# Output projections of a cross-attention layer as three products of two-part operands, with a new order of the work around them

## The reference, cut to what matters

```python
# first layer, 16 heads of width 16
y = ln(x);  x = x + softmax(q(y) k(y)^T * 64**-0.5) v(y) @ Wo1 + bo1       # self-attention
y = ln(x);  x = x + softmax(q(y) k(ctx)^T * 64**-0.5) v(ctx) @ Wo2 + bo2   # attention to the context
h, g = split(ln(x) @ Wff1 + bff1)                                         # 2 x 1024 columns
x = x + (h * (g * sigmoid(1.702 * g))) @ Wff2 + bff2
# second layer, one head of width 256, keys and values from the context
a = softmax((x @ Wq + bq) (ctx @ Wk + bk)^T / 16) (ctx @ Wv + bv) @ Wfc + bfc
out = norm_w * (x + a) * rsqrt(mean((x + a)**2) + 1e-8)
```

## Time and profile before

| | us |
|---|---|
| runs | 743.69, 746.25, 746.22; median 746.22 |
| profiled execution, its own time | 746.0 |
| its span, first to last instruction | 743.6 |
| TensorE busy | 658.1 (89%) |
| VectorE busy | 541.3 (73%) |
| ScalarE busy | 487.8 (66%) |
| GpSimd busy | 99.2 (13%) |

### The profile page before, as it was taken

How to read it: one execution, slowest core, us unless ns; L and a number is a source line. 1 busy time by engine, 2 the same in 40 slices (tenths; PEclk the granted TensorE clock), 3 DMA queues, 4 the chain that set the end, 5 groups by cost and what they waited for, 6 DMA issues and landing times.

```text
span 743.6 us, 11160 instructions
## 1 busy us (share of the span) xinstructions
PE 658.1 (89%) x4072; PEld 317.0 (43%) x4072; DVE 541.3 (73%) x929; ACT 487.8 (66%) x853; POOL 99.2 (13%) x152
## 2 busy tenths in 40 slices
PE   3989799999999999999999886778799999999981
PEld 2644122222222222222224333425458888888870
DVE  6678989999999999999993637736853944344367
ACT  3543389999999999999998662547374233332374
POOL 2071710000000000000000201345110110000004
PEclk9999699999999999999999997989999999999995
DMA  9448350202020110100000021021000000000003
GB/s 304 182 138 280 96 203 1 72 1 71 2 72 2 33 41 1 30 2 29 2 2 1 14 92 39 17 86 45 2 2 1 0 1 1 1 1 1 1 0 113
DMA packets 35113, 36.87 MB, mean 50 GB/s; under 512 B 6132, under 2 KB 28276, under 8 KB 34804
## 3 DMA queue, kind: packets, MB, share of 16 engines
q1 hardware_dynamic: 33904, 35.87, 14.7%
q0 software_dynamic: 1024, 0.24, 0.3%
q10 hardware_dynamic: 132, 0.07, 0.0%
HBM read 23.09 MB, written 12.74 MB: 48 GB/s over the span
## 4 chain that ended last, share of the span: by engine, by line
PE 63%; DVE 18%; ACT 11%; issue 5%; DMA 1%; POOL 1%; SPq 0%; ACTq 0%; DVEq 0%; POOLq 0%
PE ps L935 15%; PE ps L923 10%; DVE mm L1560 7%; PE ps L719 6%; ACT probs L1318 5%; PE ps L1121 4%; PE ps L752 4%; PE ps L1122 4%; PE ps L1123 4%; PE ps L896 3%; PE ps L705 2%; DVE tok L1538 2%; PE ps L727 2%; PE ps L1038 2%; PE ps L1137 2%
## 5 line engine op out<-in xcount | busy, mean ns | idle before, releaser
L1318 ACT ACTIVATE probs<-ps,unfit 128x512 f32<-128x512 f32 x512 | 311.3, 691 | 29.0 <-PE ps L923 24.2
L1560 DVE TENSOR_REDUCE mm<-ps 128x2 f32<-128x1024 f32 x256 | 299.5, 1220 | 13.8 <-PE ps L752 9.8
L923 PE MATMUL ps<-stack 50*128 50x512 f16 x512 | 146.9, 388 | 7.1 <-ACT probs L1318 1.2
L935 PE MATMUL ps<-probs,v 128*32 128x512 f32 x1024 | 137.3, 608 | 2.6 <-ACT outT L1323 2.6
L752 PE MATMUL ps<-stack 48*128 48x512 f16 x512 | 108.6, 391 | 12.6 <-DVE mm L1560 6.6
L923 PEld LDWEIGHTS ps<-stack 50*128 50x128 f16 x512 | 36.9, 93 | 172.4 <-ACT probs L1318 164.4
L1418 ACT ACTIVATE early<-ps,cols 128x512 f32<-128x512 f32 x32 | 22.0, 688 | 89.8 <-PE ps L1123 89.8
L1819 DVE SCALAR_TENSOR_TENSOR hid<-ps,cols,early 128x512 f32<-128x512 f32 x32 | 24.0, 750 | 72.2 <-PE ps L1123 72.2
L1373 ACT ACTIVATE probs<-ps,unfit 96x1024 f32<-96x1024 f32 x32 | 35.5, 1109 | 34.2 <-PE ps L1029 34.1
L612 POOL TENSOR_TENSOR x<-x,rows 128x512 f32<-128x512 f32 x24 | 31.9, 1340 | 150.6 <-DVE tok L1538 150.5
L1121 PE MATMUL ps<-x_hi,wff_hi 128*128 128x512 f32 x128 | 51.4, 401 | 0.0
(11 more groups left out here) (168 smaller groups left out, 868.9 us busy)
## 6 DMA issues: line engine op xcount, KB each, us to landing
v_groups<-early SPq DMA_DIRECT2D x8, 512.0 KB, 3.4
stack<-q_parts SPq DMA_DIRECT2D x64, 64.0 KB, 2.0
v<-v_groups SPq DMA_DIRECT2D x8, 512.0 KB, 4.0
x<-in_x SPq DMA_DIRECT2D x4, 512.0 KB, 7.7
q_parts<-probs SPq DMA_DIRECT2D x8, 256.0 KB, 3.8
k_parts<-probs SPq DMA_DIRECT2D x8, 256.0 KB, 2.5
stack<-k_parts SPq DMA_DIRECT2D x16, 128.0 KB, 2.5
stack<-q_parts SPq DMA_DIRECT2D x64, 32.0 KB, 1.8
```

Source lines behind the costliest of these rows:

```text
L923: eng.matmul(ps[:, st_bank(n), :], stack[rows_of(tile, KROWS), SLOTS + slot, q, P * kc:P * kc + P], qs[rows_of(tile, KROWS), slot, half, q ...
L935: mm_ = eng.matmul(ps[32 * h:32 * h + 32, PV, :], v1[:, G % 2, kc, 32 * h:32 * h + 32], probs[:, k % 2, h, :], start=(kc == 0), stop=(kc = ...
L1318: eng.activation(probs[:, k % 2, HEADS[h], :], ps[:, st_bank(n), :], ACT.Exp, scale=unfit[:, 0:1]).then_inc(exp_done, 1)
L1560: eng.tensor_reduce(dst, ps[:, 2 * slot:2 * slot + 2, :], AX.X, ALU.max).then_inc(s_red, 1)
```

## The change

- Products: the attended values are kept as a high part (att_hi, written by the ACT copies in fp32r) and a low part (att_lo, a new subtraction on DVE, attended_low, which reads the turn's PSUM banks). The two output weights are split into high and low parts on POOL (wo_split). A tile is then six fp32r products instead of two in fp32. The low parts lie over p1T, so p1T is cleared later, after the last y of the attentions is added. A turn now waits for the subtraction that reads the banks before it.
- Norm: tick() takes a count. A chain's tile calls tick(4) once (before: tick() of four steps up to four times, one of them after the yield); reduce_2 and attended_2 call tick(2).
- Order: the start of the context attention on DVE interleaves the pieces of chain(0, 1) with the first reduces; three set-up products come earlier (SETUPS); load_max_2(2) comes ahead of two stores.
- Tail: the final scaling of blocks 1 to 3 is one DVE operation per tile; ACT and POOL do block 0 alone; the roots of blocks 2 and 3 are computed together; the order of turns, squares and exponentials changes, and the last block is sent before block 2.

```diff
-        attT = (wkv1, wkv2)
...
+        att_hi = [over(f"att_hi{i}", t, [P, NC, BLK], F32R) for i, t in enumerate(("wkv1", "wkv2"))]
+        att_lo = [over(f"att_lo{i}", "p1T", [P, NC, BLK], F32R, NC * BLK * 4 * i) for i in range(2)]
+        wo_hi = [over(f"wo_hi{i}", "early", [P, NC, D], F32R, (5 * NC * D + (4 + 2 * i) * D) * 4) for i in range(2)]
+        wo_lo = [over(f"wo_lo{i}", t, [P, NC, D], F32R) for i, t in enumerate(("wo1", "wo2"))]
...
-        SETUPS = {(2, 3): 1, (3, 1): 1, (3, 3): 1, (4, 0): 1, (7, 0): 1, (7, 1): 2, (7, 2): 1, (7, 3): 1}
+        SETUPS = {(2, 2): 1, (2, 3): 2, (3, 1): 1, (7, 0): 1, (7, 1): 2, (7, 2): 1, (7, 3): 1}
...
             load_max_2(1)
+            load_max_2(2)
             for u in range(half, half + NC):
                 store_parts(u)
-            load_max_2(2)
...
-            for blk in range(BLOCKS):
-                if blk < BLOCKS - 1:
-                    eng.wait_ge(l_out, TPB * (blk + 1))
+            for n, blk in enumerate((0, 1, BLOCKS - 1, 2)):
+                if n == 0:
+                    eng.wait_ge(l_out, TPB)
                 else:
-                    eng.wait_ge(l_last, TPB)
+                    eng.wait_ge(l_last, TPB * n)
...
-            alone(eng.memset(p1T[:, :, :], 0.0))
...
+                    for s in range(2):
+                        eng.wait_ge(v_out[s], 16 * TILES // 4)
+                    for i, w in enumerate((wo1, wo2)):
+                        eng.wait_ge(w_in[("wo1", "wo2")[i]], 16)
+                        eng.tensor_copy(wo_hi[i][:, :, :], w[:, :, :]).then_inc(wo_split, 1)
+                        eng.wait_ge(wo_split, 2 * i + 1)
+                        eng.tensor_tensor(wo_lo[i][:, :, :], w[:, :, :], wo_hi[i][:, :, :].bitcast(F32), ALU.subtract).then_inc(wo_split, 1)
...
-            for blk in range(BLOCKS - 1):
-                for i in range(TPB * blk, TPB * blk + TPB):
-                    eng.wait_ge(l_scaled, i + 1)
-                    eng.tensor_tensor(x[:, i, :], x[:, i, :], rows[:, ROW_W, :], ALU.mult).then_inc(l_out, 1)
+            eng.wait_ge(y_added, 2 * TILES)
+            eng.memset(p1T[:, :, :], 0.0).then_inc(p1T_clear, 1)
+            for i in range(TPB):
+                eng.wait_ge(l_scaled, i + 1)
+                eng.tensor_tensor(x[:, i, :], x[:, i, :], rows[:, ROW_W, :], ALU.mult).then_inc(l_out, 1)
...
                     eng.wait_ge(turn_done, 2 * k)
+                    eng.wait_ge(att_lo_done, BLOCKS * n + 2 * b + (blk % 2 if phase in (ATT1, ATT2) else 2))
...
-                turned(att, 2 * b + 1)
+                eng.wait_ge(att_lo_done, BLOCKS * n + 2 * b + 2)
...
                     for c in range(NC):
-                        mm_ = eng.matmul(ps[:, out_bank(k), 0:D], attT[i // TPB][:, c, P * t:P * t + P], w[:, c, :],
-                                         start=(c == 0), stop=(c == NC - 1))
+                        hi, lo = (v[i // TPB][:, c, P * t:P * t + P] for v in (att_hi, att_lo))
+                        eng.matmul(out, hi, wo_hi[n][:, c, :], start=(c == 0), stop=False)
+                        eng.matmul(out, hi, wo_lo[n][:, c, :], start=False, stop=False)
+                        mm_ = eng.matmul(out, lo, wo_hi[n][:, c, :], start=False, stop=(c == NC - 1))
...
+            l1_turn(last)
             l1_weigh(2)
-            l1_turn(last)
...
+            l1_squares(0)
             l1_turn_copy(2)
-            l1_squares(0)
             l1_exps(last)
+            l1_turn_copy(last)
             l1_squares(1)
-            l1_turn_copy(last)
             l1_scale(0)
             l1_squares(2)
-            l1_scale(1)
             l1_squares(last)
-            l1_scale(2)
...
+            def attended_low(n, blk):
+
+                eng.wait_ge(turn_done, 2 * TURNS.index(((ATT1, ATT2)[n], blk)) + 2)
+                eng.tensor_tensor(att_lo[blk % 2][:, :, :], ps[:, CHAIN:CHAIN + NC, :], att_hi[blk % 2][:, :, :].bitcast(F32),
+                                  ALU.subtract).then_inc(att_lo_done, 1)
+
             def chain(n, b):
-                for _ in range(2):
+                for i in range(2):
+                    attended_low(n, 2 * b + i)
                     yield
                 for i in range(KC):
                     blk, t = divmod(KC * b + i, TPB)
                     add(n, KC * b + i)
-                    tick()
                     if t > 0:
                         eng.wait_ge(y_added, TILES * n + KC * b + i)
                         stats(n + 1, blk, t - 1)
-                        tick()
...
-                    tick()
+                    tick(4)
                     yield
-                    tick()
...
             reduce_2(0, 0)
+            advance(after_self, 1)
             reduce_2(0, 1)
             attended(2 * GROUPS - 1, MISC)
-            after_self, after_cross = chain(0, 1), chain(1, 0)
             reduce_2(0, 2)
+            advance(after_self, 1)
             reduce_2(0, 3)
-            advance(after_self, 4)
+            advance(after_self, 2)
...
+            def l1_final(blk, roots):
+                eng.wait_ge(l_root, roots)
+                for t in range(TPB):
+                    y = x[:, TPB * blk + t, :]
+                    eng.scalar_tensor_tensor(out=y, in0=y, scalar=rms[:, blk, t:t + 1],
+                                             in1=rows[:, ROW_W, :], op0=ALU.mult, op1=ALU.mult).then_inc(l_last, 1)
...
-            l1_root(0)
+            l1_root(0, 1)
             l1_residual(2)
-            l1_root(1)
             l1_residual(last)
-            l1_root(2)
-            l1_root(last)
...
+            l1_root(1, 2)
+            l1_final(1, 2)
+            l1_root(2, BLOCKS)
+            l1_final(last, 3)
+            l1_final(2, 3)
```

More of the change, by code:

```diff
@@ L879, in chain @@
             def chain(n, b):
-                att, ln, w = ((ATT1, LN2, wo1), (ATT2, LN3, wo2))[n]
-                eng.wait_ge(w_in[("wo1", "wo2")[n]], 16)
+                att, ln = ((ATT1, LN2), (ATT2, LN3))[n]
+                eng.wait_ge(wo_split, 2 * n + 2)
                 if (n, b) == (0, 0):
@@ L894, in chain @@
                     t = i % TPB
+                    out = ps[:, out_bank(k), 0:D]
                     for c in range(NC):
-                        mm_ = eng.matmul(ps[:, out_bank(k), 0:D], attT[i // TPB][:, c, P * t:P * t + P], w[:, c, :],
-                                         start=(c == 0), stop=(c == NC - 1))
+                        hi, lo = (v[i // TPB][:, c, P * t:P * t + P] for v in (att_hi, att_lo))
+                        eng.matmul(out, hi, wo_hi[n][:, c, :], start=(c == 0), stop=False)
+                        eng.matmul(out, hi, wo_lo[n][:, c, :], start=False, stop=False)
+                        mm_ = eng.matmul(out, lo, wo_hi[n][:, c, :], start=False, stop=(c == NC - 1))
                     mm_.then_inc(y_full, 1)
@@ L1492, in _, with tick @@
             under_way = [iter(())]
-            def tick():
-                for _ in range(4):
+            def tick(n):
+                for _ in range(n):
                     next(under_way[0], None)
@@ L1763, in reduce_2 @@
                                   AX.X, ALU.max).then_inc(s2_red, 1)
-                tick()
+                tick(2)
                 if m == KC // 2 - 1:
@@ L1789, in _ @@
                         advance(tail, TAIL[k - LEAD])
+            after_self, after_cross = chain(0, 1), chain(1, 0)
             reduce_2(0, 0)
+            advance(after_self, 1)
             reduce_2(0, 1)
             attended(2 * GROUPS - 1, MISC)
-            after_self, after_cross = chain(0, 1), chain(1, 0)
             reduce_2(0, 2)
+            advance(after_self, 1)
             reduce_2(0, 3)
-            advance(after_self, 4)
+            advance(after_self, 2)
             reduce_2(1, 0)
@@ L1846, in l1_residual, with l1_root @@
                                              in1=x[:, n, :], op0=ALU.mult, op1=ALU.add).then_inc(l_y, 1)
-            def l1_root(blk):
-                eng.wait_ge(l_sq, TPB * (blk + 1))
-                for _ in root_steps(ss1[:, blk, :], rms[:, blk, :], ms[:, blk, :], half_ms[:, blk, :], 1.0 / D, RMS_EPS, l_root):
-                    pass
+            def l1_root(first, end):
+                eng.wait_ge(l_sq, TPB * end)
+                for _ in root_steps(*(v[:, first:end, :] for v in (ss1, rms, ms, half_ms)), 1.0 / D, RMS_EPS, l_root):
+                    pass
+            def l1_final(blk, roots):
[4 more added lines that the diff above has]
+                                             in1=rows[:, ROW_W, :], op0=ALU.mult, op1=ALU.mult).then_inc(l_last, 1)
             last_piece, after_cross = after_cross, chain(1, 1)
@@ L1877, in _ @@
             l1_residual(1)
-            l1_root(0)
+            l1_root(0, 1)
             l1_residual(2)
-            l1_root(1)
             l1_residual(last)
-            l1_root(2)
-            l1_root(last)
-            eng.wait_ge(l_root, BLOCKS)
-            for t in range(TPB):
-                y = x[:, TPB * last + t, :]
```

(4 more changed lines are left out.)

6 lines of the change are left out of this document (4 added, 2 removed).

## The result

The changed kernel takes 757.41 us (median of four runs, 753.5 to 758.8) against 746.24 of the kernel before in the same comparison: ratio 1.0111, 95% interval 1.0064 to 1.0158. It is slower, and outside the predicted range of 741 to 753. Run again later beside 28 runs of the kernel before, it took 755.68 against 750.78: 1.0073 (1.0047 to 1.0100). Both intervals lie above 1: it is slower, by 1.1 and by 0.7%.

A forecast was written before the change was run, and what follows sets the result against it. TensorE, VectorE and ScalarE bound self-attention, TensorE 598 to 708 us; elsewhere the wait that ends last decides. 746.0 us and -0.5 - 0.3 + 0.5 + 6.0 - 0.9 - 3.0 = +1.8 gave 747.8, range 741 to 753.

The forecast's parts named there:

- The end of self-attention: Self-attention's last products: shorter products gain, partly eaten by waits for VectorE; net -0.5 us (-1.2 to +0.2).
- the third norm's second block: Before feed-forward: four tiles left behind the first hidden product delay TensorE's second chunk by 4.1 us.
- the second turn: Feed-forward's last chain: the second of two back-to-back turns waits 1.3 us more, for the subtraction.
- Last hidden product less first chunk: Feed-forward with the third norm's second block: 4.1 + 0.9 + 1.3 - 0.3 = +6.0 us (4.5 to 7.5).
- The tail: Kernel's end: fewer slowed VectorE operations and one joint root, against two more blocks finished on VectorE; -3.0 us.
- the start, both blocks and the transfer: Context attention's start, first layer's third and fourth blocks, maxima transfer: +2 if the clock falls, otherwise -1.4; taken as -0.3.
- so that turn ends about where it did: First layer's fourth block, 12 of 16 norm steps done when due: its turn still ends at 483.6 us.
- the 3.74 us of TensorE before 535.49 become two shorter gaps: Second attention: TensorE's one wait splits into two shorter ones; the stretch was taken as +0.5 us (-0.5 to +2).
- Transfer and set-up products: Earlier maxima transfer removes a 1.71 us wait, counted -1.4; set-up products moved into a waiting unit, -0.9 (-1.4 to 0).
- the clock stays high: Rival, faster: portions keep TensorE fed, so the other 6.8 us of lost clock return; 741 us, chance 0.23.
- The new waits cost their upper ends: Rival, slower: start and first layer +2, second attention +2, feed-forward 7.5; 753.1 us, chance 0.26.
- weight loads set the pace: Rival: each tile loses 0.27 us instead of winning 0.15, over some 10 uncovered tiles; 752.0 us, chance 0.03.

The follow-up runs named there:

- e17: The changed kernel run again without any edit, beside later runs of the kernel before: 755.68 us, ratio 1.0073.
- e5: The kernel before with the changed tail alone: 747.82 us, ratio 0.9945.
- e6: The kernel before, order untouched, with idle-time products on TensorE in four of its own waits: 742.05 us, ratio 0.9927.
- e7: The changed kernel with idle-time products on TensorE in eight of its waits: 747.77 us, ratio 0.9988 to the kernel before.
- e11: The mended kernel of e10 with idle-time products in five of its remaining waits: 727.52 us, ratio 0.9697 to the kernel before.
- e1: The changed kernel with 24 idle-time products in two TensorE waits at the start of the context attention: 754.25 us, ratio 1.0066 to the kernel before.
- e13: The changed kernel with the fourth block's norm (first layer) finished ahead of the first query remainder: 751.17 us, ratio 1.0032 to the kernel before.
- e14: The changed kernel with the four tiles of the third norm's first block behind the last reduce of the maxima: 751.53 us, ratio 1.0018 to the kernel before.
- e15: The changed kernel with the third group's maxima transfer and three set-up products back in their old places: 756.65 us, ratio 1.0105 to the kernel before.
- e8: The changed kernel with two pairs' second turns in banks of their own and the first subtraction later: 749.58 us, ratio 1.0023 to the kernel before.
- e3: The changed kernel with the third norm's second block finished ahead of the first hidden product, behind the last attended output: 758.21 us, ratio 1.0103.
- e9: The changed kernel with the third norm's second block finished ahead of the last attended output: 751.70 us, ratio 1.0035 to the kernel before.
- e10: The changed kernel with the edits of e8, e9, e13 and e14 together, no idle-time products: 733.72 us, ratio 0.9764 to the kernel before.

## Why the prediction was wrong

**What held.** The products lie 0.118 us apart at full clock (586.06, 586.17, 586.29 in the trace), with a load of 0.19 each: the earlier trace rows carried over. The end of self-attention is +0.8 at 391 us and +0.3 at 437, so -0.5 as summed. The largest single term, the third norm's second block, was predicted at +4.1 and is +4.3 (in e17 too); the clock behind it (0.9) 1.1; the second turn (1.3) 1.3. Last hidden product less first chunk: +15.8 - 9.5 = +6.3, predicted +6.0 (+8.9 in e17, above the 7.5 of its range, as the clock stayed low for longer behind the two waits). The tail is -3.8 by both traces and by e5, predicted -3.0.

**The step that failed** is the price of the clock, above all in the context attention, 438 to 554 us: -0.3 + 0.5 - 0.9 = -0.7 in the sum, +9.5 - 0.3 = +9.2 in the trace. That is 9.9 of the 10.2 us by which the traces miss the sum. How much falls there is partly the luck of one execution: in e17's trace the same stretch is +3.1, with +1.6 ahead of it, +8.9 in the feed-forward and -3.8 in the tail. Four of its steps:

- *"If the clock falls there, these parts come to +2; if not, -1.4. I take -0.3 for the start, both blocks and the transfer."* The first wait was sized right (first scores 1.0 later, as worked out), and of the 5.7 us at the first transposed scores some 2.8 are waits, where 2.0 (1.0 to 2.5) was estimated. But the clock was priced as one fork in one stretch. It fell at the first wait and again at three later ones; over the stage 16.8 us more of it were lost than before, in e17 6.7 more. e6, e7 and e11 show that it costs by itself, e1 that it is half of the first 5.7 us.
- *"so that turn ends about where it did".* It ended at 488.0, not at 483.6 (in before the next scores waited for a transfer until 485.33, so they start 2.6 later); e13 shows that the place of these steps costs some 4.5.
- *"the 3.74 us of TensorE before 535.49 become two shorter gaps".* They became two gaps, of 1.45 and 2.59, together no shorter (1.45 and 3.74 in e17), because the four tiles still stood ahead of the last reduce; behind them the clock fell to 0.57. e14 moves the tiles and gains 4.2, though before had the same order and lost 3.74 to it.
- *Transfer and set-up products, -1.4 and -0.9.* TensorE no longer waits for the third group's maxima, but it doesn't in e15 either, and e15 can't find the gain. The next wait, for the transfer of the queries, is 2.12 before, 4.30 in the trace above, 2.03 in e17 and 4.37 in e13; what sets it was not tested.

**The base.** The sum was made against 746.0, one of the quicker executions of before (clock 0.965). In 92 later runs its median was 750.7. The same sum on that would be 752.5; the changed kernel measured 755.7. So of some 12 us between the two traces about half is chance: the trace of before was one with little lost clock, and that of the change one of its slower executions. Lost clock differs by 40.9 - 33.6 = 7.3 us over all 11 runs of the changed kernel; at 0.5 to 0.7 that is 3.7 to 5.1 of the 6.6 us between the mean spans. The rest, 1.5 to 2.9, is near the +1.8 of the sum. That is not a proof of its terms: the sum has some clock in it (0.9 behind the first chunk, a share of the -0.3), and its terms missed in both directions.

**The rivals.** That the clock stays high (chance 0.23) was the opposite of what came: it was 0.79 from 450 to 545 us, 0.86 in e17, 0.89 before. "The new waits cost their upper ends" came nearest (753.1), by the clock more than by the waits. That weight loads set the pace is ruled out by the spacing. What stays open: how much each wait must shrink before the clock holds (a wait of 1.28 at the start left it at 1.00, yet four of 0.49 to 1.63 behind it in e8 were followed by 0.62), and what the products alone are worth.

## What to carry to other kernels

Where TensorE waits between bursts, price the low clock behind every wait, not at one of them, and take the base of a sum from several executions with their granted clocks. Before a step is moved in an engine's order, look for the next wait in that order: e3 put the work one line too late and gained nothing, e9 one line earlier and gained 4.0 of the 4 to 5 expected. When a subtraction reads a bank that a later turn needs, another bank can be cheaper than any order (e8).

## What the runs showed of the hardware

- Products of the identity with itself, whose results nobody reads, made the kernel before 1.1% faster in the median (e6) and the mended one 0.8% (e11 against e10). Lost clock fell by 12.7 and 13.4 us with it. Behind the filled stalls that ended at 458 and 535 the clock was 1.00 in e6; it still fell to 0.66 from 500 to 515 in e11.
- TensorE was busy 11.12 of 13 us from 445 to 458 at a clock of 0.51, and 12.92 of 13 from 462 to 475 at the same level, both behind waits (2.38 us ahead of 444.88; 0.95 and 0.66 around 460): the low clock lasted through work that was hardly interrupted. The Trainium skill (TensorE: Matmul & The Clock Gate, "HAM oscillation — how this bites in real kernels") describes bursts between waits for transfers that each begin at the low clock. This trace agrees, with VectorE as what is waited for ahead of 444.88.
- The kernel before spread over 742.5 to 753.2 us in 92 runs, in step with its mean granted clock (0.966 to 0.949; 1.1 us of scatter about the line). Two executions of the changed kernel differ by 6.1 us in the context attention alone, at 0.76 and 0.85.
